# A two-layer graph network on one core: own parts on four PSUM banks, and a last block that sums its high parts first

## The reference

```python
Wh = x @ W.T
sim = Wh @ Wh.T / (norms * norms.T + EPS)
alpha = softmax(where((adj > 0) | eye, sim, -inf), axis=1)
x1 = layernorm(x + alpha @ Wh)
```

```python
deg = sum(mask, axis=1)
agg = mask @ x1 / maximum(deg, 1)
combined = concat([x1 @ W_self + b_self, agg @ W_nb + b_nb])
out = layernorm(x1 + relu(combined @ W_comb + b_comb))
```

## Time and profile before

| | us |
|---|---|
| median of 3 runs | 901.79 |
| lowest and highest | 901.30, 901.96 |
| the profiled execution | 900.57 |
| its span, first to last instruction | 898.8 |
| TensorE busy | 877.6 (98%) |
| VectorE busy | 588.0 (65%) |
| ScalarE busy | 391.1 (44%) |
| GpSimd busy | 64.2 (7%) |

### The profile page before, as it was taken

One profiled execution on the slowest core, in us unless ns is written; L12 is line 12 of the kernel. 1 busy time (PEld: TensorE's weight loads), 2 busy tenths in 40 slices (PEclk: granted clock), 3 DMA queues, 4 the chain that ended last, 5 costly groups with the idle time before them and its releaser, 6 DMA issues.

```text
span 898.8 us, 20852 instructions
## 1 busy us (share of the span) xinstructions
PE 877.6 (98%) x7151; PEld 711.1 (79%) x7151; DVE 588.0 (65%) x1265; ACT 391.1 (44%) x661; POOL 64.2 (7%) x175
## 2 busy tenths in 40 slices
PE   7989999999999999999999999999999999999997
PEld 6857777687777777787777777777888888888886
DVE  3787788887766777668868777889816333333333
ACT  4955655565665656565556665555310000000000
POOL 2300000000000000000000000011101000000000
PEclk9999999999999999999999999999999999999999
DMA  9226455465555654567558559584773213312200
GB/s 243 99 83 172 131 170 147 122 192 159 145 153 160 192 149 145 168 175 187 162 145 229 148 157 305 160 223 109 207 115 115 96 43 112 113 50 80 112 19 18
DMA packets 143213, 128.29 MB, mean 143 GB/s; under 512 B 64225, under 2 KB 120834, under 8 KB 142114
## 3 DMA queue, kind: packets, MB, share of 16 engines
q1 hardware_dynamic: 143058, 127.20, 49.5%
q0 software_dynamic: 80, 0.13, 0.1%
HBM read 95.83 MB, written 25.18 MB: 135 GB/s over the span
## 4 chain that ended last, share of the span: by engine, by line
issue 87%; POOL 5%; PE 4%; DMA 1%; DVE 1%; POOLq 1%; ACT 0%; SPq 0%; DVEq 0%
POOL rstd L527 3%; PE ps L1061 3%; POOL var_eps L525 1%; DMA feat<-xT 1%; PE ps L1073 1%; PE ps L1116 0%; POOLq L526 0%; PE ps L1143 0%; DVE work L692 0%; POOLq L524 0%; DVE work L807 0%; ACT prob_hi L593 0%; DVE big L685 0%; DVE mix_extremes L764 0%; POOLq L529 0%
## 5 line engine op out<-in xcount | busy, mean ns | idle before, releaser
L1165 PE MATMUL ps<-feat,prob_hi 128*128 128x257 f16 (+1 forms) x1024 | 279.8, 273 | 0.0
L1167 PE MATMUL ps<-feat,prob_lo 128*128 128x257 f16 (+1 forms) x1024 | 279.5, 273 | 0.0
L1166 PE MATMUL ps<-feat,prob_hi 128*128 128x256 f16 (+1 forms) x1024 | 278.9, 272 | 0.0
L839 DVE SCALAR_TENSOR_TENSOR prob_lo<-work,prob_hi 128x512 f16<-128x512 f32 x256 | 175.9, 687 | 82.1 <-ACT prob_hi L593 79.7
L1298 PE MATMUL ps<-big,mgroup 128*128 128x257 f16 x1024 | 226.2, 273 | 0.0
L1299 PE MATMUL ps<-big,mgroup 128*128 128x256 f16 x1024 | 226.2, 273 | 0.0
L593 ACT ACTIVATE prob_hi<-work 128x512 f16<-128x512 f32 x256 | 154.5, 624 | 91.2 <-DVE work L832 46.0
L586 ACT ACTIVATE work<-ps 128x512 f32<-128x512 f32 (+2 forms) x144 | 79.5, 556 | 138.1 <-PE ps L1095 120.6
L598 ACT ACTIVATE mask<-work 128x1024 fp8e4<-128x1024 f32 x128 | 133.5, 1043 | 0.0
L1166 PEld LDWEIGHTS ps<-feat,prob_hi 128*128 128x128 f16 x1024 | 100.3, 98 | 25.1
L1165 PEld LDWEIGHTS ps<-feat,prob_hi 128*128 128x128 f16 x1024 | 100.0, 98 | 24.2 <-issue 0.3
(11 more groups left out here) (121 smaller groups left out, 788.9 us busy)
## 6 DMA issues: line engine op xcount, KB each, us to landing
adj_sb<-adjT SPq DMA_DIRECT2D x128, 512.0 KB, 3.8
mask_spill<-mask SPq DMA_DIRECT2D x128, 128.0 KB, 2.7
mgroup<-mask_spill SPq DMA_DIRECT2D x8, 2048.0 KB, 8.3
xres<-x SPq DMA_DIRECT2D x8, 512.0 KB, 5.0
x1h_dram<-big SPq DMA_DIRECT2D x16, 256.0 KB, 5.2
out<-rows SPq DMA_DIRECT2D x32, 128.0 KB, 1.7
feat<-xT SPq DMA_DIRECT2D x7, 512.0 KB, 5.8
norm_bc<-norm_row_dram SPq DMA_DIRECT2D x8, 256.0 KB, 4.9
```

The lines of the kernel that those rows point to most:

```text
L839: dve.scalar_tensor_tensor(out=prob_lo[:, s, :], in0=prob[:, s, :], scalar=PROB_SCALE, in1=prob_hi[:, s, :], op0=ALU.mult, op1=ALU.subtrac ...
L1165: pe.matmul(acc(D + 1), prob_hi[:, s, cols], feat_hi_of(g)[:, r, 0:D + 1], start=start, stop=False)
L1166: pe.matmul(acc(D), prob_hi[:, s, cols], feat_lo_of(g)[:, r, :], start=False, stop=False)
L1167: return pe.matmul(acc(D + 1), prob_lo[:, s, cols], feat_hi_of(g)[:, r, 0:D + 1], start=False, stop=stop)
```

## The change

Three things. The own parts go round banks 0 to 3 by b % 4, and own(b) waits only until the own part of block b - 4 has been read. For the last block, 31, TensorE no longer alternates: it sums all 32 high parts in bank 7, raises the new semaphore last_hi_done, and then sums all 32 low parts in bank 0, after a wait for the own part of block 28, which lay there. VectorE makes deg, reciprocal and a first blend of the last block from the high sum after last_hi_done, and when agg_done comes it adds the low sum times rdeg with one more instruction. The other blocks are computed as before.

```diff
         def own_ps(b):
-            return ps[:, b % 2, 0:D]
+            return ps[:, b % GB, 0:D]
+
+        def last_lo_ps():
+            return ps[:, 0, 0:D]
...
+        last_hi_done = sem("last_hi_done")
...
                 y = summed[:, q, 0:D]
-                dve.wait_ge(agg_done, b + 1)
+                dve.wait_ge(last_hi_done if b == NB - 1 else agg_done, 1 if b == NB - 1 else b + 1)
...
                 dve.wait_ge(blend_ready, b + 1)
+                if b == NB - 1:
+                    dve.wait_ge(agg_done, NB)
+                    chain.join(chain.step(dve.scalar_tensor_tensor(out=y, in0=last_lo_ps(), scalar=rdeg[:, q:q + 1], in1=y,
+                                                                   op0=ALU.mult, op1=ALU.add)))
...
                 pe.wait_ge(x1T_loaded[g], 16 * 2)
-                wait(pe, own_ready, b - 1)
+                wait(pe, own_ready, b - GB + 1)
...
+            def add_last(b):
+
+                q, slot = b % GB, b // GB % 2
+                cols = lambda jb: mgroup[:, slot, jb * GW + q * P:jb * GW + (q + 1) * P]
+                for jb in range(NB):
+                    ins = pe.matmul(agg_ps(q, D + 1), cols(jb), z_hi_of(jb // GB)[:, jb % GB, 0:D + 1], start=(jb == 0), stop=(jb == NB - 1))
+                ins.then_inc(last_hi_done, 1)
+                pe.wait_ge(own_ready, b - GB + 2)
+                for jb in range(NB):
+                    ins = pe.matmul(last_lo_ps(), cols(jb), z_lo_of(jb // GB)[:, jb % GB, :], start=(jb == 0), stop=(jb == NB - 1))
+                ins.then_inc(agg_done, 1)
...
+                elif b < NB - 1:
+                    add_neighbours(b, range(G // 2))
                 else:
-                    add_neighbours(b, range(G // 2))
-                if b + 1 < NB:
-                    own(b + 1)
+                    add_last(b)
+                    break
+                own(b + 1)
                 add_neighbours(b, range(G // 2, G))
```

## The result

| | before | after |
|---|---|---|
| median, 13 runs each, us | 902.02 | 899.59 |
| lowest and highest, us | 900.68 to 903.44 | 898.52 to 900.55 |
| the profiled execution, us | 900.57 | 898.79 |
| its span, us | 898.8 | 897.0 |
| instructions of VectorE | 1265 | 1266 |

The ratio of after to before is 0.9983, with a 95% interval of 0.9975 to 0.9990: 0.17% less, or 1.5 us of 902. By this ratio the kernel is a little faster, by less than the 0.2% that I had set as the bound for telling it from no change. The two medians lie further apart, 2.43 us or 0.27%; why the ratio on record is nearer to one isn't known.

A forecast was written before the change was run, and what follows sets the result against it. The prediction took TensorE, busy 98% of the span, to set the pace. It summed 1.17 us before own(6) and 0.51 us after the last matmul to 1.68, giving 901.79 - 1.68 = 900.11 us, range 899.2 to 901.3.

The forecast's parts named there:

- The sum: Whole kernel: 1.17 us from TensorE's gap before own(6) plus 0.51 us after the last matmul, 1.68 us saved.
- The hole: TensorE before own(6), 688.72 to 690.00 us: waits for own_out(4), queued behind VectorE's backlog; four banks save 1.17 us.
- Nothing late next: TensorE after own(6): no later blend, mask load or own-part wait takes back the 1.17 us.
- The last block: Block 31, split into high and low parts: the chain after the last matmul falls from 1.03 to 0.52 us, saving 0.51.
- the new instruction starts where deg did: VectorE after the last matmul: the added blend takes deg's start time and L1026 follows 0.52 us later.
- Cost: 0: TensorE in block 31: the new order of 64 matmuls and the wait between halves add no time.
- one of my signs: End of the changed kernel: new instruction within 0.05 us of the last matmul, L1026 0.52 us later.
- The cover for the first blend: Block 31 on VectorE: deg, reciprocal and first blend finish by 891.0 us, 2 us before the low parts end.
- deg and the reciprocal: VectorE's tail: rows show 0.51 us from deg to blend; the skill's estimate gives 0.19; the rows were to decide.
- The wait only moves: Rival, chance 0.07: TensorE is held soon after own(6) by something else, leaving only 0.51 us saved, 901.3 us.
- the tail gives nothing: Rival, chance 0.07: after the last matmul, a second wait or late high part cancels the 0.51 us, 900.6 us.
- The slower one, by the clock: Rival, chance 0.03: TensorE pauses at bank changes in the own parts and its clock falls; 903.6 us or more.

The follow-up runs named there:

- alone: Four banks for the own parts, last block unsplit, against the kernel before: own(0) to end 1.21 us shorter, ratio 0.9987.
- another run: Kernel before (two banks, old last block) with each own part from block 5 on issued at its block's start: ratio 1.0066, 5.1 us slower in the trace.
- the two series: The changed kernel timed twice against the kernel before, the second time beside another follow-up kernel on the same chip: ratios 0.9983 and 0.9977.

## Why the prediction was right, point by point

- **The sum.** Predicted 1.68 us; the ruler gives 1.59 and 1.57, the ratios 1.5 and 2.1 us (0.17% and 0.23%). The time, 899.59, lies inside the range, but 0.5 us under the forecast, and for no reason that I gave: the median of the kernel before was itself 0.23 higher in the longer series than in the three runs that I started from, and the medians fell by 2.43 us, 0.8 more than the traces account for. I take the rest for scatter, which isn't shown. I had put the scatter at some 0.5 us from three runs that lay 0.66 apart; 13 of them lie 2.76 apart.
- **The hole.** Predicted 1.17, measured 1.21 alone and 1.59 - 0.42 = 1.17 in the changed kernel. The cause was right, VectorE's backlog in front of own_out(4): moving that one instruction removes the hole without a bank, and asking for the bank 3.50 or 1.75 us earlier lengthens it by just that.
- **Nothing late next.** Right: no gap in TensorE's starts after 640 us. One detail was off: deg of block 5 moved by 0.82 us (694.36 - 670.87 against 693.33 - 670.66) where I had allowed 0.74, because it needn't wait for the end of own_out(5) as drawn. Nothing hangs on it.
- **The last block.** Predicted 0.51, measured 0.40 to 0.43. The step that failed is "the new instruction starts where deg did", together with "Cost: 0" for the new order. Each had a small price: 0.06 to 0.07 us for the order of the waits, some 0.05 for sorting the parts. 0.51 - 0.07 - 0.05 = 0.39. The rows of VectorE say the same without a span: from the start of the last matmul to the activation it is 894.11 - 892.77 = 1.34 us before, 892.34 - 891.44 = 0.90 after, and 893.75 - 892.92 = 0.83 with the waits swapped, which is the 0.51 less that I had predicted. So one of my signs missed: the new instruction was to start within 0.05 us of the last matmul, as deg did (0.04 behind its drawn end), and starts 891.83 - 891.71 = 0.12 behind it. The reading that a met wait costs TensorE nothing was circular as I made it (the step divided by 70), but the rows around own(6) bear it out. The cover for the first blend was there: VectorE stood idle 2.37 us ahead of L1032.
- **deg and the reciprocal.** Here the rows and the page differed: the estimate from the table of the Trainium skill (VectorE: DVE Perf Modes, "The TRN2 errata") made the term 0.19. Measured is 0.4, and 0.50 with the waits swapped (17.10 - 16.60), so the measurement decides for the rows. The estimate is too low for each of the two instructions: it has 0.13 and 0.06 us, and the rows of the kernel before draw deg with 0.28 and the reciprocal, at 893.39, with 0.16.
- **The rivals.** "The wait only moves" and "the tail gives nothing" are both out: the hole is gone and the tail is 0.42 us shorter. The slower one, by the clock, didn't come: four banks go round with a clock of 1.00 and no pause, so the failure that the Trainium skill tells of (TensorE: Matmul & The Clock Gate, "A second HAM failure mode: psum-queue depth-cycling") has no counterpart here. That idle time can cost clock in this stage is seen in another run: behind the hole of 4.68 us it fell.
- **The bound.** I said that the forecast lay just on the near side of 0.2%. The ratios of the two series fall on either side of it, 0.17% and 0.23%, and the medians of the first lie beyond it, 0.27%. The traces put the change at 1.59 us, 0.18%. So timing alone doesn't decide on which side it lies.

## What to carry to other kernels

An engine that waits for a buffer may be waiting for a reader that stands behind other work in an in-order queue; look at what is ahead of the reader before adding buffers, since moving one small copy gave the same 1.2 us here as two more banks. For changes under the scatter of the timing, measure in the trace from a landmark behind the unchanged part: here that takes out 2 us of scatter and leaves some 0.05, the rounding of the span. And when an instruction on the critical tail has two waits, put the one that is met last first; here that was worth 0.07 us at the start of the instruction.

## What the runs showed of the hardware that I had not expected

- A wait of TensorE costs more than its length once the clock falls: after holes of 1.17 and 2.91 us the granted clock stayed at 1.00, after one of 4.68 us it averaged 0.57 over the next 4 us and cost 1.6 us more. Each is one trace.
- 32 matmuls of 257 columns one behind another start 0.1116 us apart, those of 256 columns 0.1090, and alternating they average 0.1095.
- VectorE starts 0.31 to 0.32 us behind the start of the last matmul when the wait for it is the only one or the first of two, and 0.37 to 0.39 when an already met wait stands ahead of it (five traces).
- The first layer alone, the same work in every run, ends at times that are up to 2.1 us apart (own(0) at 670.00 to 672.14 us). What in it varies wasn't looked into.
